# One table of times that orders an attention part over five engines: new times for its steps

## The reference

```python
x = x + xattn(ctx, layernorm(x), mask, mask, W_src, b_src, W_tgt, b_tgt, W_out, b_out)
x = x + ffn(layernorm(x), gate_w, w_gate, w_up, w_down, sw_gate, sw_up, sw_down)

# xattn: k, v from ctx; q from the normed x; 8 heads of 32
scores = einsum('bthd,bshd->bhts', q, k) / sqrt(32)      # masked keys: -inf
update = einsum('bhts,bshd->bthd', softmax(scores), v)
return concatenate([tgt, update]) @ W_out.T + b_out
# ffn: 16 experts, top 8 of sigmoid(l2norm(x) @ l2norm(gate_w).T), weights normed, + a shared one
h = silu(x @ w_gate[e]) * (x @ w_up[e]) * weight[e];  y += h @ w_down[e]
```

## Time and profile before

| what | us |
|---|---|
| median of the three runs | 1054.44 |
| the profiled execution's own time | 1049.61 |
| its span, first to last instruction | 1047.5 |
| PE busy | 1003.0 |
| VectorE, ScalarE, GpSimd busy | 655.4, 467.2, 389.4 |
| granted clock of TensorE, mean share | 0.989 |

### The profile page before, as it was taken

The page is one execution under the profiler, slowest core; times in us unless marked ns, Lnnn a source line. Parts: engine busy times, 40 slices in busy tenths (PEclk is TensorE's granted clock), DMA queues, the critical chain, the costliest instruction groups (busy, mean ns, idle before and its releaser), DMA issues.

```text
span 1047.5 us, 14744 instructions
## 1 busy us (share of the span) xinstructions
PE 1003.0 (96%) x5070; PEld 761.4 (73%) x5070; DVE 655.4 (63%) x1510; ACT 467.2 (45%) x881; POOL 389.4 (37%) x355
## 2 busy tenths in 40 slices
PE   4889999999999998899999999999999999999998
PEld 3656767676767664567888888888888888888886
DVE  6866767776767577445665566556556556555544
ACT  3447565666565646445424333333333333333322
POOL 2569797879797967345310010010010100100000
PEclk9999999999999997999999999999999999999999
DMA  7543342424242223325333232242341232332230
GB/s 232 131 132 93 101 132 67 128 72 134 70 114 70 65 64 101 81 81 122 95 72 68 52 81 58 54 82 50 63 80 42 71 82 46 74 75 60 67 72 24
DMA packets 84377, 87.87 MB, mean 84 GB/s; under 512 B 13160, under 2 KB 66296, under 8 KB 84304
## 3 DMA queue, kind: packets, MB, share of 16 engines
q1 hardware_dynamic: 82384, 84.85, 32.9%
q10 hardware_dynamic: 1920, 2.10, 0.6%
HBM read 56.99 MB, written 4.46 MB: 59 GB/s over the span
## 4 chain that ended last, share of the span: by engine, by line
PE 89%; DVE 5%; ACT 2%; SPq 1%; issue 1%; POOL 1%; DMA 1%; DVEq 0%; ACTq 0%; POOLq 0%
PE ps L659 49%; PE pst L659 18%; PE ps L765 5%; PE ps L738 5%; PE pst L754 5%; PE ps L665 4%; DVE mx L1196 1%; PE ps L778 1%; SPq L611 1%; SPq L546 1%; ACT e_buf L866 1%; DVE lg L1277 1%; ACT ctx_h L866 0%; DVE wsrc_l L1145 0%; DMA x<-in_x 0%
## 5 line engine op out<-in xcount | busy, mean ns | idle before, releaser
L659 PE MATMUL ps<-x_h,weights 128*128 128x512 f32 x1088 | 365.6, 397 | 2.8 <-DVE sg L1297 2.0
L659 PEld LDWEIGHTS ps<-x_h,weights 128*128 128x128 f32 x1088 | 204.4, 188 | 52.7 <-issue 2.5
L1196 DVE TENSOR_REDUCE mx<-ps 128x1 f32<-128x512 f32 x256 | 173.2, 684 | 95.4 <-PE ps L738 94.8
L659 PE MATMUL ps<-x_l,weights 128*128 128x512 f32 x544 | 214.5, 394 | 0.0
L866 ACT ACTIVATE hh<-qb 128x512 fp32r<-128x512 f32 x136 | 86.0, 632 | 287.7 <-DVE qb L1311 268.2
L659 PE MATMUL pst<-hh,weights 128*128 128x512 f32 x544 | 193.2, 397 | 0.0
L866 ACT ACTIVATE e_buf<-pst 128x512 f32<-128x512 f32 x256 | 147.1, 595 | 100.4 <-PE pst L754 90.5
L1300 DVE TENSOR_TENSOR qb<-ps,sg 128x512 f32<-128x512 f32 x136 | 94.0, 691 | 135.9 <-PE ps L659 132.2
L1316 DVE TENSOR_TENSOR hl<-qb,hh 128x512 fp32r<-128x512 f32 x136 | 94.3, 693 | 92.2 <-ACT hh L866 92.0
L1406 POOL TENSOR_TENSOR e_sums<-e_sums,e_buf 128x1024 f32<-128x1024 f32 x60 | 143.4, 2390 | 8.6 <-ACT e_buf L866 2.5
L1358 POOL TENSOR_SCALAR ve<-mv 128x4 f32<-128x4 f32 x8 | 1.8, 229 | 337.8 <-DVE mv L1238 337.8
(11 more groups left out here) (154 smaller groups left out, 1360.7 us busy)
## 6 DMA issues: line engine op xcount, KB each, us to landing
cb<-combine_scratch SPq DMA_DIRECT2D x128, 256.0 KB, 4.7
q_stack<-q_h SPq DMA_DIRECT2D x128, 64.0 KB, 2.0
k_stack<-k_h SPq DMA_DIRECT2D x124, 64.0 KB, 2.0
ctx_raw<-in_ctxT SPq DMA_DIRECT2D x7, 1024.0 KB, 5.3
q_stack<-q_l SPq DMA_DIRECT2D x64, 64.0 KB, 2.0
out_x<-ob SPq DMA_DIRECT2D x16, 256.0 KB, 2.1
k_stack<-k_l SPq DMA_DIRECT2D x62, 64.0 KB, 2.0
x<-in_x SPq DMA_DIRECT2D x7, 512.0 KB, 6.8
```

The source lines that it names most:

```text
L659: ins = engine.matmul(dst, lhsT, rhs, start=start and n == 0, stop=stop and n == len(terms) - 1)
L1196: engine.tensor_reduce(MX[:, g % 2, h // 2, h % 2, q:q + 1], bank(step), AX.X, ALU.max).then_inc(sem("max"), 1)
```

## The change

The two constants for the lead of maxima and scores go, and nearly every step gets a time of its own: in `project` the first and second group of a context may differ, the opening list becomes single steps half a tick apart, each of a context's four copies has a number, maxima run at 1.0 ticks in the first group, 0.95 in the middle ones and 1.02 in the last, and the tables of the last three groups change. No instruction is added, removed or altered, and the code that the engines run is the same. SyncE's order stays. The core of the diff:

```diff
-        at(t + (2.5 if half == 0 else 0.2), ("q", p))
+        at(t + (2.49 if half == 0 else 0.99), ("q", p))
...
-        at(t - 0, ("turn_x", b, 1))
-        at(t - 0, ("hi_x", b, 1))
-        at(t - 0, ("lo_x", b, 1))
+        at(t - 0.82, ("turn_x", b, 1))
+        at(t - 1.11, ("hi_x", b, 1))
+        at(t - -0.12, ("lo_x", b, 1))
...
-    at(-42.4, *first)
+    at(-49.0, ("ctx", 0, 0))
+    at(-46.75, ("ctx", 0, 1))
+    at(-48.0, ("turn_x", 0, 0))
+    at(-47.5, ("hi_x", 0, 0))
...
-    at(-9.1, ("y", 0, 0, 1))
+    at(-3.17, ("y", 0, 0, 1))
-    at(-6, ("k", 1, 0))
-    at(-4.9, ("k", 1, 1))
+    at(-9.2, ("k", 1, 0))
+    at(-6.0, ("k", 1, 1))
...
-    for j in range(16 * NG):
-        at(j - MAX_LEAD, ("max", j // 16, j // 4 % 4, j % 4))
+    for g in range(NG):
+        for n in range(16):
+            when = -14.1 + 1.0 * n if g == 0 else -14.0 + 0.95 * n if g < NG - 1 else -14.0 + 1.02 * n
+            at(16 * g + when, ("max", g, n // 4, n % 4))
...
-            at(16 * g + 8 * a - 5.4, ("shift", g, a))
-            at(16 * g + 8 * a - 4.9, ("neg", g, a))
+            at(16 * g + 8 * a - 5.04, ("shift", g, a))
+            at(16 * g + 8 * a - 4.43, ("neg", g, a))
...
-                at(t + (2.7, 2.8, 5.9, 11.2, 14.3, 15.8)[3 * a + i], ("e_add", g, a, i))
+                at(t + (3.1, 3.45, 5.9, 13.99, 14.3, 15.8)[3 * a + i], ("e_add", g, a, i))
...
-        at(t + 21.2, ("recip", g))
+        at(t + 20.8, ("recip", g))
...
-            at(t - 0 + 0.8 * k, ("ctx", c, k))
+            at(t + (0.1, 0.56, 1.6, 2.3)[k], ("ctx", c, k))
...
-        at(t + (2.6 + 0.3 * i if i < 10 else 8 + 0.33 * (i - 10)), s)
+        at(t + (0.05 + 0.33 * i if i < 10 else 8 + 0.19 * (i - 10)), s)
...
-    for n, when in enumerate((3.6, 7.2, 13, 16.2, 25.3, 26.6)):
-        at(t + when + 0.5, ("silu", n))
+    for n in range(FIRST_UNITS):
+        at(t + (2.6, 7.29, 13.09, 16.29, 24.91, 26.69)[n], ("silu", n))
```

More of the change, by code:

```diff
@@ L126, in attention @@
-    at(-42.4, *first)
+        at(t - 0.82, ("turn_x", b, 1))
+        at(t - 1.11, ("hi_x", b, 1))
+        at(t - -0.12, ("lo_x", b, 1))
+    for i, s in enumerate([("first_loads",), ("ones",), *chain("ln1", N_FIRST1 + 4, 0)]):
+        at(-60 + 0.05 * i, s)
+    at(-50.0, ("wt_hi",))
+    at(-49.5, ("wt_lo",))
+    at(-49.0, ("ctx", 0, 0))
+    at(-46.75, ("ctx", 0, 1))
+    at(-48.0, ("turn_x", 0, 0))
+    at(-47.5, ("hi_x", 0, 0))
+    at(-47.0, ("turn_x", 0, 1))
+    at(-46.5, ("hi_x", 0, 1))
@@ new lines, in attention @@
+    at(-46.46, ("lo_x", 0, 0))
+    at(-45.5, ("lo_x", 0, 1))
+    at(-45.0, ("ctx", 0, 2))
+    at(-44.5, ("ctx", 0, 3))
+    at(-42.74, ("ws_hi", 0))
+    at(-43.5, ("q", 0))
+    at(-44.9, ("ws_lo", 0))
+    at(-42.5, ("out_q", 0))
+    at(-42.0, ("hi_q", 0))
+    at(-41.5, ("load_ctx", 1))
+    at(-41.0, ("k", 0, 0))
+    at(-40.5, ("k", 0, 1))
+    at(-40.0, ("mask_bias",))
+    at(-39.5, ("ws_hi", 1))
+    at(-39.0, ("hi_k", 0))
+    at(-38.5, ("ws_lo", 1))
+    at(-38.0, ("lo_k", 0))
+    at(-37.87, ("bias_row", 0))
@@ L127, in attention @@
+    at(-37.0, ("stack", 0, 0))
+    at(-36.5, ("stack", 0, 1))
+    at(-36.0, ("stack", 0, 2))
+    at(-35.5, ("stack", 0, 3))
+    at(-36.63, ("wo",))
+    at(-38.12, ("q", 1))
+    at(-33.2, ("bv",))
+    at(-33.5, ("v", 0, 0, 0))
+    at(-33.0, ("v", 0, 0, 1))
+    at(-32.5, ("out_q", 1))
+    at(-32.0, ("bo",))
+    at(-31.5, ("out_v", 0, 0))
+    at(-31.0, ("bias_row", 1))
     for i, s in enumerate(chain("ln1", N_LN1, 1)):
-        at(-26.2 if i < 30 else -14.8 + 0.25 * (i - 30), s)
-    at(-14, ("v", 0, 1, 0))
+        at(-30.68 if i < 30 else -14.24 + 0.24 * (i - 30), s)
@@ L149, in attention @@
     for g in range(NG):
         for a in range(2):
[L151 to L152 removed]
+            at(16 * g + 8 * a - 5.04, ("shift", g, a))
+            at(16 * g + 8 * a - 4.43, ("neg", g, a))
     for m in range(2 * NU):
[L154 removed]
+        g, n = divmod(m, 16)
+        at(16 * g + (-1.5 + 1.0 * n if g < NG - 1 else -1.47 + 1.0 * n), ("scores", m))
     for g in range(NG):
@@ L201, in attention @@
     for i, s in enumerate(chain("gating", N_GATE, 0)):
-        at(t + (4.3 + 0.3 * i if i < N_TANH else 7 + 0.3 * (i - N_TANH)), s)
+        at(t + (4.53 + 0.3 * i if i < N_TANH else 7 + 0.3 * (i - N_TANH)), s)
     at(t + 12.4, ("turn_c", 0))
-    at(t + 13.5, *[("load_c", m) for m in range(NC)])
+    at(t + 13.65, *[("load_c", m) for m in range(NC)])
     t = 16 * (NG - 1)
```

90 lines of the change are left out of this document (42 added, 48 removed).

## The result

The changed kernel takes 1030.35 us (median of 4 runs, 1029.46 to 1030.86) against 1053.51 us of the kernel before on the same chip: ratio 0.9777, 95% interval 0.9759 to 0.9796, so 23.2 us or 2.2% faster. The forecast was 1043, range 1035 to 1054: the sign was right, the gain was twice the 11.4 us that I said. The profiled executions are 1029.46 and 1049.61 us, 20.15 apart.

A forecast was written before the change was run, and what follows sets the result against it. Only PE's waits and lower-clock stretches in the first 475 us could gain. Terms, including +0.2 for the last normalisation, sum to -11.4: 1049.61 to 1038.2 us profiled, carried over to the 1054.44 median as 1043; range 1035 to 1054.

The forecast's parts named there:

- The steady contexts: Six contexts: projection q covers the wait before score 36, a shorter one comes before 35; -2.1 us, bounds 0 and -6.6.
- The second norm's copies: Groups 13 and 14: GpSimd's norm chain ends before its sum, copies go ahead of an exponential; -2.0 us, bounds -4.5 and +1.
- Gating: Group 14: a gating step put ahead of the next maximum makes that maximum late by the tanh; +0.4 us, bounds 0 and +1.5.
- y in the gap: Last groups: twelve y matmuls fill PE's wait for a maximum at 421.53, at the higher clock; -3.0 us, bounds -1.4 and -3.5.
- the rule I weighed: VectorE 2-port and GpSimd instructions exclude each other; a gating step ahead of a maximum may stand a whole GpSimd instruction; priced 0.4 us.
- First units: Units 0 to 3: ScalarE does the tanh sooner, so PE's waits go; -3.5 us, bounds -1.5 and -4.2.
- Start: Opening: q 0.3 us late, then waits for k's high part and the mask bias row go; -1.4 us, bounds +0.8 and -2.5.
- rival 1: Last groups: the clock stays up, so two remaining half-clock stretches go, another 5 us, 1038 us; chance 0.12.

The follow-up runs named there:

- e5: Kernel before with only the changed project, next_x and times of a context's four copies (the context's turn): 1048.22 us, ratio 0.9945.
- e4: Kernel before with only maxima 0.95 of a tick apart ahead of the last group, and shift and neg later: 1050.98 us, ratio 0.9964.
- e9: Kernel before with the edits of e5 and e4 together, nothing else: 1042.51 us, ratio 0.9887.
- e2: Kernel before with only the last groups' edits: 1047.52 us, ratio 0.9932.
- e8: Kernel before with the edits of e2 and e_add's three new times: 1040.53 us, ratio 0.9886.
- e7: Changed kernel with the second norm's chain back at its old times: 1030.41 us, ratio 0.9787.
- e10: Changed kernel with the last group's maxima 1 tick apart again, so y stands behind the maximum: 1031.56 us, ratio 0.9788.

## Why the prediction was wrong, step by step

The forecast lies 8.8 us above the profiled execution (1038.2 against 1029.46) and 12.7 above the median. The range was wrong by its own terms too: their lower bounds add up to -21.1 us, which is 1033 and not 1035; the median lies below both.

- **The steady contexts: the failed step, -2.1 forecast, -7.6 measured (5.5 us).** "A wait of 0.75 us goes, 0.5 to 0.8 come". The new wait is where I put it, before score 35, 67, and is shorter:

```profile
92.79 0.65 ACT L903 ACTIVATE ctx_h<-ctx_raw 128x512 fp32r<-128x512 f32 x1
```
```profile
92.98 0.50 PE L791 MATMUL pst<-q_stack,k_stack 98*128 98x512 f32 x1 [0.32 <-ACT e_buf L903]
```

  As the worth of the turn alone, -2.1 was right (e5: 2.14). What failed is that the maxima and the shift have no term in the sum, and no reason is given for it. Alone they are worth 0.6 (e4), with the turn they add 5.3 (e9). The 0.6 was there to be seen: the view of the earlier trace rows has a second row, the 0.9 us for `gate_sb` shown above, and my list of places has only the six waits for exponentials. The 5.3 no row shows. My bound of -6.6, "no wait is left", was too narrow too, since it counted the six waits and not the small stalls under the list.
- **The second norm's copies: -2.0 against -4.7.** The sequence was as told: chain ended before the sum, score 224 waiting, less than counted; but the lower clock of the earlier trace rows did not come, which I had as a bound of -4.5:

```profile
379.34 0.24 POOL L1415 TENSOR_SCALAR rn<-v 128x4 f32<-128x4 f32 x1
379.67 2.39 POOL L1443 TENSOR_TENSOR e_sums<-e_buf 128x1024 f32<-128x1024 f32 x1
```
```profile
382.32 0.47 PE L791 MATMUL pst<-q_stack,k_stack 98*128 98x512 f32 x1 [0.87 <-ACT e_buf L903]
```

  Most of it is e_add's place (from e2 to e8 4.3 us more by attend (13,1)), not the chain's own times (e7: 1.0 there, 1.6 by the end).
- **Gating: +0.4 against -1.6.** The wait at the maximum fell from 2.09 to 1.06 us instead of growing: the gating step of 1.55 us of the earlier trace rows takes 0.35 us at its new place. And the stretch of lower clock at 411.2 is 3.4 us long at 396.2 now.
- **y in the gap: -3.0 against -1.5.** y stands in the gap at full clock, worth 2.8 in e10's trace. But part of it was taken back one maximum earlier: the wait of PE at (15,2,3), ahead of y, grew from 0.52 to 2.28 us, while the one at (15,3,0) fell from 2.04 to 0.60:

```profile
404.56 0.50 PE L775 MATMUL ps<-k_stack,q_stack 97*128 97x512 f32 x1 [2.28 <-DVE mx L1233]
...
407.33 0.47 PE L775 MATMUL ps<-k_stack,q_stack 97*128 97x512 f32 x1 [0.60 <-DVE mx L1233]
```

  This is the rule I weighed and then priced on the wrong instruction. The long step of the earlier trace rows is short now. Three of the four products between 400.5 and 406.6 are long (1.16, 2.39 and 2.02 us), each until a GpSimd instruction ends (401.58, 403.88, 406.42), and the maxima stand behind them. They were as long in the kernel before, one row from the one that I quoted (last line):

```profile
L1314 DVE TENSOR_SCALAR lg<-sc,ts x32: 223/231/2394, 400.5 to 932.8; 128x16 f32<-128x16 f32 x32
L1294 DVE TENSOR_TENSOR lg<-lt x8: 224/226/355, 393.9 to 923.7; 128x64 f32<-128x64 f32 x8
```
```profile
L1277 DVE TENSOR_SCALAR lg<-sc,ts x32: 222/230/2401, 414.6 to 952.9; 128x16 f32<-128x16 f32 x32
```

- **First units: -3.3 against -3.14**, unit 3's wait 0.63 us where 2.05 stood. **Start: -1.4 against -1.56**, in part luck: score 12 waits 2.60 us, a microsecond more than before where half of one was told, and the other five profiles with the same start are 2.0 to 2.5 us ahead at score 28.
- **The clock stays up** (rival 1, 0.12): it largely did, beside the other terms. The kernel before has a mean granted clock of 0.9854 over the 63 timed runs beside the experiments, the changed one 0.9943 over its four. Over those 63 runs, 0.001 of mean clock goes with 0.65 us (correlation -0.82; 0.59 us within a group of runs), which would make 5.8 of the 23.2 us. No experiment moves the clock alone, so this share is an estimate.
- **From profile to median: 3.9 us.** I carried the 4.8 us between the profiled execution and the median over to the changed kernel; it has 0.9. The profiled execution of before had a clock of 0.989 where the runs have 0.985, by the slope above 2.3 of those us. It shows no lower clock between 20 and 58 us; of nine other profiles with at least a part of the old opening or old context times, eight have 3.4 to 6.8 us of it between 42 and 52 (e9 has none). None of the six profiles with the changed kernel's start does.

## What to carry to other kernels

Edits of an order are not priced one by one by the row of waits that each removes: two that gave 2.1 and 0.6 us alone gave 7.5 together, because each left stalls at places that the other covers. Where a change moves several engines' work in one period, lay one whole period of both orders side by side, sum distances from step to step (not only the listed waits), and reach the range to the case in which all stalls go. And what one edit gives alone can come from one odd place: the 0.6 us came from one context in six. Before the difference between a profiled execution and the median is carried over, ask whether it is the clock: here it went from 4.8 to 0.9 us with a change that shortened waits.
